# Summing eight terms on VectorE: three additions in place of one summing instruction, in the first round of an expert stage

## The reference, cut to what matters

```
kv  = einsum('bhil,bhjl->bijhl', k, v)            # all products of two components of a head
y   = irfft(rfft(kv, 2L) * rfft(ssm_kernel, 2L))  # causal convolution along the sequence
out = einsum('bijhl,bhil->bjhl', y + kv * D, q)   # for each j: the sum over i of eight terms
x   = x + tanh(g_xattn[1]) * out
```

## Time and profile before

| | |
|---|---|
| median of 3 runs | 2029.07 us (2028.69 to 2031.53) |
| the profiled execution | 2031.29 us, span of its instructions 2029.5 us |
| mean granted TensorE clock | 0.975 |
| TensorE busy | 1920.4 us (95%) |
| VectorE busy | 1484.9 us (73%) |
| ScalarE busy | 1027.9 us (51%) |
| GpSimd busy | 1037.0 us (51%) |
| the summing instruction (L2277), all rounds | 124 times, 256.6 us |

### The profile page before, as it was taken

The page is one execution under the profiler, slowest core; times in us unless marked ns, Lnnn a source line. Parts: engine busy times, 40 slices in busy tenths (PEclk is TensorE's granted clock), DMA queues, the critical chain, the costliest instruction groups (busy, mean ns, idle before and its releaser), DMA issues.

```text
span 2029.5 us, 27663 instructions
## 1 busy us (share of the span) xinstructions
PE 1920.4 (95%) x10020; PEld 1565.7 (77%) x10050; DVE 1484.9 (73%) x2229; ACT 1027.9 (51%) x1468; POOL 1037.0 (51%) x788
## 2 busy tenths in 40 slices
PE   6999769999997669999999999999999999999998
PEld 5888746666653658888888888888888888888886
DVE  5877569888884777867876976876886787687422
ACT  4447547776764435336337427335434633733532
POOL 1110144444430856665666665666565566576554
PEclk9999889999999779999999999999999999999999
DMA  5866415566645113324244233242332423421422
GB/s 196 312 239 230 180 47 136 145 164 172 148 112 131 62 33 129 95 84 147 72 120 131 73 119 107 96 126 79 130 105 87 142 70 112 146 78 63 135 99 68
DMA packets 170115, 249.72 MB, mean 123 GB/s; under 512 B 91356, under 2 KB 92764, under 8 KB 163708
## 3 DMA queue, kind: packets, MB, share of 16 engines
q1 hardware_dynamic: 169692, 247.86, 39.7%
q10 hardware_dynamic: 288, 0.10, 0.0%
HBM read 193.13 MB, written 33.69 MB: 112 GB/s over the span
## 4 chain that ended last, share of the span: by engine, by line
PE 61%; POOL 2%; DVE 1%; issue 1%; DMA 1%; SPq 0%; DVEq 0%; ACT 0%; POOLq 0%; ACTq 0%
PE e_ps_u L54 6%; PE e_ps_out L54 6%; PE e_ps_u L55 6%; PE e_ps_u L56 6%; PE e_ps_out L56 6%; PE e_ps_out L55 6%; PE e_ps_g L55 4%; PE e_ps_g L56 4%; PE e_ps_g L54 4%; PE e_ps_m L56 4%; PE e_ps_m L55 4%; PE e_ps_m L54 4%; PE e_ps_m L2873 1%; DMA e_dn_raw<-in_md 1%; PE e_ps_m L2827 1%
## 5 line engine op out<-in xcount | busy, mean ns | idle before, releaser
L1418 POOL TENSOR_TENSOR e_gu_lo<-e_gu_raw,e_gu_hi 128x1024 fp32r<-128x1024 f32 (+1 forms) x128 | 287.8, 2251 | 176.0 <-ACT e_gu_hi L1722 175.5
L2277 DVE TENSOR_REDUCE e_x3T<-e_zp 128x128 f32<-128x1024 f32 x124 | 256.6, 2070 | 6.4 <-ACT x_held L1837 5.3
L1423 POOL TENSOR_TENSOR e_dn_lo<-e_dn_raw,e_dn_hi 128x512 fp32r<-128x512 f32 x128 | 183.8, 1438 | 110.2 <-ACT e_dn_hi L1728 109.4
L54 PE MATMUL e_ps_u<-e_xn_hi,e_gu_hi 128*128 128x512 f32 x512 | 203.3, 397 | 0.0
L54 PE MATMUL e_ps_out<-e_hd_hi,e_dn_hi 128*128 128x512 f32 x512 | 201.8, 394 | 0.0
L55 PE MATMUL e_ps_u<-e_xn_lo,e_gu_hi 128*128 128x512 f32 x512 | 199.9, 390 | 0.0
L56 PE MATMUL e_ps_u<-e_xn_hi,e_gu_lo 128*128 128x512 f32 x512 | 199.8, 390 | 0.0
L56 PE MATMUL e_ps_out<-e_hd_hi,e_dn_lo 128*128 128x512 f32 x512 | 199.6, 390 | 0.0
L55 PE MATMUL e_ps_out<-e_hd_lo,e_dn_hi 128*128 128x512 f32 x512 | 199.5, 390 | 0.0
L2209 DVE TENSOR_TENSOR e_hd_lo<-gate_held,e_hd_hi 128x512 fp32r<-128x512 f32 x128 | 146.6, 1145 | 70.2 <-ACT e_hd_hi L1752 70.0
L1439 POOL TENSOR_TENSOR e_kv_raw<-e_ke 128x512 f32<-128x512 f32 x128 | 148.2, 1158 | 82.5 <-DVE e_kv_lo L2241 76.9
(11 more groups left out here) (316 smaller groups left out, 5070.3 us busy)
## 6 DMA issues: line engine op xcount, KB each, us to landing
e_gu_raw<-in_mgu SPq DMA_DIRECT2D x96, 512.0 KB, 3.8
e_dn_raw<-in_md SPq DMA_DIRECT2D x128, 256.0 KB, 2.8
e_wb<-wts SPq DMA_DIRECT2D x8, 1536.0 KB, 7.2
c<-in_ctxT SPq DMA_DIRECT2D x8, 1024.0 KB, 7.7
raw_w<-in_w1T SPq DMA_DIRECT2D x8, 1024.0 KB, 4.9
x_held<-in_w2T SPq DMA_DIRECT2D x8, 1024.0 KB, 7.4
gates<-gate_held SPq DMA_DIRECT2D x8, 1024.0 KB, 5.6
vals<-o SPq DMA_DIRECT2D x8, 1024.0 KB, 4.9
```

The costliest lines, as they stand in the source:

```text
L54: nc.tensor.matmul(out, w_hi, x_hi, start=first, stop=False, skip_group_check=skip)
L1418: nc.gpsimd.tensor_tensor(gu_lo[:, s % 2, a], gu_raw[:, s % 2, a], f32(gu_hi[:, s % 2, a]), ALU.subtract).then_inc(gulo_done, 1)
L1423: nc.gpsimd.tensor_tensor(dn_lo[:, s % 2], dn_raw[:, s % 2], f32(dn_hi[:, s % 2]), ALU.subtract).then_inc(dnlo_done, 1)
L2277: nc.vector.tensor_reduce(x3T[:, lb].rearrange("p (b n) -> p b n", b=B)[:, :, hh * CD:(hh + 1) * CD], zv(5, (1, 8), (21, 8)), AX.X, ALU.ad ...
```

## The change

In round 0, and there alone, `add_terms` on VectorE sums by halves: it adds the last four terms to the first four (128 x 512), of these the last two to the first two (128 x 256), and the last two into `x3T` (128 x 128). Each addition reads two tensors in SBUF; the first two write in place in `zp`. A new semaphore, `halves_done`, orders the three among themselves. The later rounds keep the summing instruction. Nothing else is changed; the name lists of the semaphores get the new name.

```diff
             dve.wait_ge(prod_done, START + 4 * (v + 1))
-            nc.vector.tensor_reduce(x3T[:, lb].rearrange("p (b n) -> p b n", b=B)[:, :, hh * CD:(hh + 1) * CD],
-                                    zv(5, (1, 8), (21, 8)), AX.X, ALU.add).then_inc(red_done, 1)
+            out = x3T[:, lb].rearrange("p (b n) -> p b n", b=B)[:, :, hh * CD:(hh + 1) * CD]
+            if q > 0:
+                nc.vector.tensor_reduce(out, zv(5, (1, 8), (21, 8)), AX.X, ALU.add).then_inc(red_done, 1)
+                return
+            terms = lambda i, n: zv(5 + 21 * i, (21, n), (1, 8))
+            done = 2 * sums(v)
+            nc.vector.tensor_tensor(terms(0, 4), terms(0, 4), terms(4, 4), ALU.add).then_inc(halves_done, 1)
+            dve.wait_ge(halves_done, done + 1)
+            nc.vector.tensor_tensor(terms(0, 2), terms(0, 2), terms(2, 2), ALU.add).then_inc(halves_done, 1)
+            dve.wait_ge(halves_done, done + 2)
+            nc.vector.tensor_tensor(out, zv(5, (1, 8)), zv(26, (1, 8)), ALU.add).then_inc(red_done, 1)
```

More of the change, by code:

```diff
@@ L1164, in experts_block @@
              "stats_done mom_done rstd_done shift_done xq_done x2T_filled x2T_done q_filled qe_done ke_done kvraw_done "
-             "kvhi_done kvlo_done td_done thi_done tlo_done unit_done prod_done red_done x3_done nat_filled pstats_done "
+             "kvhi_done kvlo_done td_done thi_done tlo_done unit_done prod_done red_done halves_done x3_done nat_filled pstats_done "
              "pmom_done prstd_done pshift_done xnat_done xnT_filled xnhi_done xn_done lgT_filled lgT_done lg_filled lg_done rt exp_done w_done "
@@ L1170, in experts_block @@
      stats_done, mom_done, rstd_done, shift_done, xq_done, x2T_filled, x2T_done, q_filled, qe_done, ke_done, kvraw_done,
-     kvhi_done, kvlo_done, td_done, thi_done, tlo_done, unit_done, prod_done, red_done, x3_done, nat_filled, pstats_done,
+     kvhi_done, kvlo_done, td_done, thi_done, tlo_done, unit_done, prod_done, red_done, halves_done, x3_done, nat_filled, pstats_done,
      pmom_done, prstd_done, pshift_done, xnat_done, xnT_filled, xnhi_done, xn_done, lgT_filled, lgT_done, lg_filled, lg_done, rt, exp_done, w_done,
```

## The result

The changed kernel takes 2039.33 us in the median of 4 runs (2038.33 to 2040.13), the kernel before 2028.99 us (2028.69 to 2031.53, 4 runs beside them): 10.3 us more, a ratio of 1.005 with an interval of 1.0038 to 1.0062. Predicted were 2040 us, in a range from 2033 to 2046.

What follows compares the result with a forecast made beforehand. GpSimd was taken to carry the first-round state-space stage up to unit 14, VectorE its last 11 us. On VectorE's queue +14.3 - 0.5 - 1.3 - 1.5 = +11.0 us on 2029.07 gave 2040 us, range 2033 to 2046.

Steps and rivals of the forecast that it cites:

- Where the end is set: From 752 to 2015 us TensorE is busy for 1262 of 1263 us, so lateness at 752 us stays to the end.
- One sum: First-round VectorE sum: three additions with waits for GpSimd take 3.36 us against 2.06, 1.30 us more each.
- GpSimd's share: GpSimd's next instruction starts 0.42, 0.20 or 0.03 us late behind 512, 256 or 128 elements, 0.65 us per sum.
- The rival that took it literally: GpSimd loses every addition's whole length, 1.43 us per sum in place of 0.65: 2045 us; chance 0.03.
- The sum of the terms: On VectorE's queue, eleven sums at +1.30 us give +14.3, the last one, without GpSimd, -0.5.
- idle time of 2.56 us: VectorE's idle time before 700.91 us takes up part of the lateness; half counted, -1.3 us.
- The two add_x2 steps: At 730.67 us, 2.92 us beside GpSimd, they will find it done and take 1.4: -1.5 us.
- The signs it named: 512-element additions mostly end 0.5 us after a GpSimd instruction; unit 14's cut_kv ends at 726 or later; x3's turn near 747.
- Only GpSimd's lateness: VectorE swallows its longer sums in idle time and waits; the chain stays GpSimd's: +4, 2033 us; chance 0.15.
- TensorE behind: Units 7 and 11 on TensorE lose +1 us each and no idle time is taken up: +14, 2043 us; chance 0.12.
- Not held up: Additions do not collide with GpSimd, each sum is 0.54 us shorter, GpSimd's chain stays: -1.1 us, 2028; chance 0.06.

Runs made afterwards that it cites:

- the kernel with inputs from PSUM: Changed kernel, but terms 3 to 6 go to PSUM and five additions of one SBUF and one PSUM input replace the three: 2029.1 us, ratio 0.9995.
- the tiny ones in a chain: Kernel before plus three 128x8 SBUF additions ahead of each first-round summing instruction, each waiting for the one before: 2045.65 us, ratio 1.0078.
- Three independent tiny ones: Kernel before plus three independent, unused 128x8 SBUF additions ahead of each of the twelve first-round summing instructions: 2039.73 us, ratio 1.0048.

## Why the prediction was right

**Where the end is set.** It said that what is late at 752 us is late at the end. The time from x3's turn to the end differs by 1.2 us between the two profiles, against 9.7 in the stage.

**One sum.** From the start of the first addition to that of VectorE's next instruction, the eleven sums with GpSimd beside them take 3.35 us on average (1.25, 1.37 and 0.66 for the additions, the rest hand-overs), from 2.13 to 4.86 in single ones; predicted were 3.36. That close an agreement is partly luck, for the pieces are off: the model had about 1.15, 1.18 and 1.00. It drew the lengths of GpSimd's instructions at random, while in the queue the long step of `pairs` is followed by its short one. The second addition mostly sits out a long step (1.15 us seven times, 2.2 beside one of GpSimd's sums three times), and the third then meets the short step and goes through bare in 8 of 12 sums. The twelfth sum took 1.51 us, predicted bare at 1.52.

**GpSimd's share.** Later by 0.45 us behind an addition of 512 elements and 0.18 behind one of 256, by its rows after; predicted were 0.42 and 0.20. The Trainium skill's page "SBUF — State Buffer", section "SBUF: two separate sides", calls the shared pair an exclusive lock that is held for a whole instruction, and names VectorE instructions with two SBUF inputs. That an input in PSUM frees the addition and GpSimd alike agrees with it (0.42 us in every one of twelve). "The whole instruction" is more than the rows bear out: an addition with a bare length of 0.68 us cost GpSimd 0.45, one of 0.43 us 0.18. The rival that took it literally, 5 us above the forecast, falls with that.

**The sum of the terms.** Eleven sums and the last, each up to VectorE's next instruction: 38.4 us in all against 24.2 before (there without the idle time of 2.56 us), +14.2; predicted +13.8. The two add_x2 steps fell from 2.92 us to 1.41: -1.5, as predicted. The mis-sized term is VectorE's idle time of 2.56 us before 700.91: I counted half of it, -1.3, because TensorE's unit 7 would wait for VectorE's product of unit 5. It does not. The code of `unit` waits until `prod_done` has counted four products for each of the first u - 2 units; that is the products of unit u - 3, and not of unit u - 2 as I had it. In the trace of before, unit 7 starts at 694.75 us, while the products of unit 5 end at 694.91, and what it had waited for is a subtraction of GpSimd:

```profile
694.75 0.61 PE L54 MATMUL e_ps_out<-e_xn_hi,e_hd_hi 128*128 128x288 f32 x1 [1.96 <-POOL e_kv_lo L1447]
```

So unit 7 became late with GpSimd, and not with VectorE: it starts 19.3 us into the stage before and 20.7 after. Its product, which had the idle time before it, now follows VectorE's sum of unit 5 without a gap:

```profile
702.84 0.29 DVE L2287 TENSOR_TENSOR e_x3T<-e_zp 128x128 f32<-128x128 f32 x1
703.17 0.69 DVE L2261 TENSOR_TENSOR e_zp<-e_ps_out,e_qe 128x512 f32<-128x512 f32 x1
```

All of it is gone, -2.6. The other two-input instructions of VectorE, and a wait of 0.17 us for TensorE that is gone too, make -0.4; the prediction had left them at nothing. 14.2 - 2.6 - 1.5 - 0.4 = 9.7, against +11.0 predicted.

**The signs it named.** Of the eleven first additions, ten end 0.5 to 0.6 us after a GpSimd instruction. Two of its times come earlier than it said: `cut_kv` of unit 14 ends at 724.76 us, not at 726 or later, and x3's turn starts at 744.41, not near 747. 1.5 us of both is the earlier start of the profiled stage; the rest of the second is mostly the idle time above.

**The rivals.** "Only GpSimd's lateness" (+4) is refuted: GpSimd is no longer on the chain, it idles 1.08 us before 729.98 for a product of VectorE, and the subtraction for unit 14 ends at 724.76, 5 us later into the stage than before, the 5.2 that its lateness was priced at, while the stage ends 9.7 later. "TensorE behind" (+14) did not occur: VectorE has no wait for TensorE behind the first product. Its condition, that a unit starts behind the products of two units earlier, is one unit too tight as well. "Not held up" (2028) is what the kernel with inputs from PSUM shows, at 2029.1, no change that can be told from its 2029.73 before. There the small price that the prediction gave it held; in the changed kernel its condition did not.

## What to carry to other kernels

An instruction with a longer bare time and one SBUF input can be cheaper than two or three short ones with two SBUF inputs each, when GpSimd's queue beside it has no gaps: price such an instruction by what is left of GpSimd's running instruction, not by its elements, and price it once for each place in the chain where the next must wait for the last (0.59 and 0.61 us on average for the tiny ones in a chain, where the bare length is 0.16). An input in PSUM took VectorE out of these turns; what that freed paid here only when the other queue of the stage got shorter too. Free time of an engine in the mean hides no lateness in places where several waits come in a row.

## What the runs showed of the hardware that I had not expected

Two independent VectorE instructions that stand ready can pass GpSimd together: in the group at 706.53 us two took their bare 0.17 and 0.16 us, and the third 1.40 behind GpSimd's next. Three independent tiny ones cost 1.26 us per sum (15.1 / 12), where three that wait for one another cost 1.81 (21.7 / 12), the hand-overs between them not counted.

The step of an access decided much of VectorE's time here. The summing instruction took 2.03 us with 21 words between its terms and 1.22 with them side by side; a product that writes 512 results took 0.69 us, and 1.15 with a step of eight words.
